# A six-layer hybrid model in one kernel: the parts of queries and keys as two float32r values in the halves of the TensorE array

## The chip, the cores and the metric

The kernel is one program on one core of a Trainium2 chip. The core has TensorE (PE) with its weight loads (PEld), VectorE (DVE), ScalarE (ACT), GpSimd (POOL) and SyncE (SP), and 16 DMA engines that the queues of SP, ACT and POOL share. The metric is the device time of one execution in microseconds (us), and the figure compared is the median of several runs. Everything is computed in this one launch.

## The reference

The input x is 2048 tokens of 128 channels. Layers are added to it one after another: softmax attention with rotary positions and a root-mean-square norm of q and k; a spline feed-forward; retention; the spline feed-forward again; linear attention; an attention with a convolution ahead of it and a mixture of four experts behind; a WKV recurrence; and the attention with experts once more. So softmax attention is computed three times and retention once. Cut to what this change touches:

```python
# softmax attention, three times: 16 heads of 8 channels, T = 2048, causal
attn = einsum('bqhd,bkhd->bhqk', q, k) * scale
attn = softmax(where(causal, attn, -inf))
out = einsum('bhqk,bkhd->bqhd', attn, v)
# retention: 16 heads, keys of 8 channels, values of 16
scores = einsum('bhtd,bhsd->bhts', q, k) * mask        # decay, causal
denom = clip(abs(scores).sum(-1), 1.0, 50000.0)
ret = einsum('bhts,bhsv->bthv', scores / denom, v)
```

## The kernel before

**Parts.** A head has only 8 channels, so its products q.k need 8 rows of the 128-row array. The kernel uses the other rows for precision: `qkv_stage` (L635) writes each transposed q and k as a sum of PARTS = 3 bfloat16 parts. ACT's `part` (L764) copies the transposed block out of PSUM as bfloat16, PE's `take_out` (L715) subtracts that copy from PSUM by a matmul with minus one, and this goes on for the second and third part; the last block's keys are cut by DVE (`keys_part`, L849). SP stores the parts to DRAM. All nine products of parts (3 x 3 x 8 = 72 = KROWS rows) are then summed by one bfloat16 matmul whose contraction runs over 128 rows: 72 of parts, two of shifts, the rest padding.

**The attention stage** (`attention_stage`, L960, about 479 us, three times) goes through 4 groups of 4 heads and 4 blocks of 512 queries, 16 units of (group, block). It has two streams. The first finds row maxima: PE's `max_unit` (L1094) makes a 128 x 512 product (`stat`, L1101) in one of three PSUM banks, and DVE's `max_unit` (L1197) reduces it, plain ones at L1209 and the diagonal ones with a mask at L1206. A bank is filled again only when DVE has left it. When a unit's maxima are there, DVE splits them in two parts, PE transposes them (L1107), and small DMAs (`load_shift_rows`, L1006) write them as two further rows of the queries, so that the next products come out already shifted. The second stream has 160 steps: per step PE makes the scores of four heads against 128 keys (`scores`, L1143, matmul L1151, two heads per PSUM tile `sc[hp]`), ACT exponentiates two heads at a time (L1087), POOL masks the diagonal (L1056), and `pv` (L1155, matmul L1164) multiplies by the values, in float32, four heads in four 32-column tiles of the array.

**The order on PE** is fixed. `attention_plan` (L917) spreads the 672 items of the first stream (the RING) evenly over the half steps; PE's loop issues, per step: wait for ACT, scores of heads 0 and 1 for the next step, its share of ring items, `pv` of the step before, wait for ACT, scores of heads 2 and 3, its share of ring items. PE issues in order, so a ring item that waits for a bank holds up everything behind it. In most units the heads of successive ring items are 0, 1, 2, 3.

**Loads.** Each group's rows come from DRAM by `load_k` and `load_q` (L95, L102) on SP's queue, the next group while a group is worked on. The first two blocks of group 0 are loaded ahead, block 0 in `qkv_stage` itself; then SP queues the other blocks, the padding of group 1 and group 1, and behind these the shift rows of the second unit.

**Retention** (`retention_heads_stage`, L1664, about 200 us) takes the heads one at a time, two buffers deep. PE makes the own (diagonal) products, 128 wide, four to a bank (L1822), and the others up to 512 wide for DVE (L1826) and up to 1024 wide for ACT (L1812); ACT and DVE sum absolute values. SP loads a head's rows by six DMAs (L1729, L1730).

Of the kernel before, what the change touches and what calls it, by code (L numbers as in the profile page):

```python
# [4 lines left out]

# [5 lines left out]
F32 = mybir.dt.float32  # L12
BF16 = mybir.dt.bfloat16
I32 = mybir.dt.int32
# [5 lines left out]
P = 128  # L20
# [6 lines left out]
PARTS = 3  # L27
KROWS = PARTS * PARTS * D
SHIFT = 2
VD = 16  # L30
HG = 4
NG = H // HG
GBUFS = 2
# [61 lines left out]
def load_k(eng, tile, k_dram, g, parts, cols, sig):  # L95

    rows = k_dram.rearrange("(g h d) a t -> g (d a) h t", h=HG, d=D)
# [4 lines left out]
def load_q(eng, tile, q_dram, g, parts, cols, sig):  # L102

    rows = q_dram.rearrange("a (g h d) c t -> a g (d c) h t", h=HG, d=D)
    for a in parts:
        eng.dma_start(tile[a * PARTS * D:(a + 1) * PARTS * D, :, cols], rows[a, g][:, :, cols]).then_inc(sig.sem, 16)

NROWS = 2 * PARTS
# [3 lines left out]
def pad_rows(eng, w, q_tile, k_tile, sig):  # L113

    for n, tile in enumerate((q_tile, k_tile)):
        eng.dma_start(tile[KROWS:P].rearrange("r h t -> r (h t)"), w["pad"][n].partition_broadcast(P - KROWS)).then_inc(sig.sem, 16)
# [23 lines left out]
def load_stage(k, d, w):  # L140

    nc = k.nc
    with ExitStack() as ctx:
# [8 lines left out]
            (w["ident"][:], d["c_ident"]),  # L152
            (w["cos"][:], d["c_cos"]),
# [4 lines left out]
        with nc.Block() as block:  # L158
# [23 lines left out]
            def _(dve):  # L182
# [4 lines left out]
                nc.vector.tensor_scalar(w["minus16"][:], w["ident"][:], -1.0, None, ALU.mult).then_inc(kept.sem, 1)  # L187
# [447 lines left out]
def qkv_stage(k, w, jobs, qkv, parts_dram, mode, turned_sb, norm, loads=(), rows=None):  # L635
# [10 lines left out]
    with ExitStack() as ctx:  # L646
# [3 lines left out]
        early = k.sb("early_parts_t", [P, 2, 2, PARTS, BANK], BF16, ctx)  # L650
        parts = [early[:, c] if c < 2 else turned_sb[:, c - 2] for c in range(NQ)]
# [33 lines left out]
        with nc.Block() as block:  # L685

            @block.tensor
            def _(pe):
# [12 lines left out]
                def turn(c):  # L701
# [4 lines left out]
                    for s in range(2):  # L706
                        nc.tensor.matmul(tp[c % 2][:, s, :], w["minus16"][:], zeros, start=True, stop=True)
# [7 lines left out]
                def take_out(c, a):  # L715

                    pe.wait_ge(cut[a].sem, cut[a].at(c + 1))
                    for s in range(2):
                        if c == NQ - 1 and s == 1:
                            pe.wait_ge(keys_cut.sem, keys_cut.at(a + 1))  # L720
                        ins = nc.tensor.matmul(tp[c % 2][:, s, :], w["minus16"][:], parts[c][:, s, a, :], start=False, stop=True, skip_group_check=True)
# [13 lines left out]
                take_out(NQ - 1, 1)  # L735

            @block.scalar
            def _(act):
# [25 lines left out]
                def part(c, a):  # L764
# [4 lines left out]
                    if c < NQ - 1:  # L769
                        ins = nc.scalar.copy(parts[c][:, :, a, :], tp[c % 2][:])  # L770
                    else:
                        ins = nc.scalar.copy(parts[c][:, 0, a, :], tp[c % 2][:, 0])
                    ins.then_inc(cut[a].sem, 1)

                for n in range(NQ):
# [3 lines left out]
                    if n > 0:  # L779
                        part(n - 1, 2)  # L780
# [5 lines left out]
                part(NQ - 1, 2)  # L786
# [5 lines left out]
            def _(dve):  # L792
# [56 lines left out]
                def keys_part(a):  # L849
# [5 lines left out]
                    nc.vector.tensor_copy(parts[NQ - 1][:, 1, a, :], tp[(NQ - 1) % 2][:, 1]).then_inc(keys_cut.sem, 1)  # L855
# [23 lines left out]
            def _(sp):  # L879
                if rows:  # L880
                    pad_rows(sp, w, *rows, padded)
                for c in range(NQ - 1 if rows else NQ):
# [5 lines left out]
                    if rows and c == 1:  # L888
                        sp.wait_ge(stored[0].sem, stored[0].at(NS))
                        load_k(sp, rows[1], parts_dram[1], 0, range(PARTS), slice(0, BANK), begun)  # L890
                        load_q(sp, rows[0], parts_dram[0], 0, range(PARTS), slice(0, BANK), begun)
                for c in range(2):
# [67 lines left out]
def attention_stage(k, w, v, parts_dram, first_rows, last_parts, scale, y, first_norm=None):  # L960
# [7 lines left out]
    ROWS = KROWS + SHIFT  # L968
    counts = []
    with ExitStack() as ctx:  # L970
        uq, uk = ([first_rows[n], k.sb(f"group_{what}", [P, HG, T], BF16, ctx)] for n, what in enumerate("qk"))
# [4 lines left out]
        mxb = k.sb("row_max_parts", [P, 2, SHIFT * HG * QC], BF16, ctx)  # L976
        mxt = k.sb("row_max_turned", [SHIFT * HG * QC, 2, P], BF16, ctx)
# [1613 lines left out]
```

## Time and profile before

| | us |
|---|---|
| median of 3 runs | 2440.61 |
| lowest and highest run | 2437.79, 2441.31 |
| the profiled execution: its span | 2438.4 |
| what lies around the span | not shown by itself; the median is 2.2 above the span |
| attention stages, PE's first to last matmul | 68.4 to 547.8, 1123.5 to 1602.5, 1840.4 to 2319.9 |
| retention heads, PE's first to last matmul | 688.0 to 888.7 |

Read the table of busy time together with the windows: an average over the whole span mixes stages with different limits. In the rows below a name such as `stat<-group_k,group_q` says which tile is written from which; PEld rows are weight loads. `first_group_q` and `group_q` are the two buffers of query rows. An "idle before" in brackets is the time the engine had stood still, and what ended it.

### The profile page before, as it was taken

To read this page: it belongs to the slowest core of one execution; us is meant where nothing else is said; L and a number is where in the kernel's file an instruction comes from. 1 tells how busy PE (TensorE), PEld (TensorE's weight loads), DVE (VectorE), ACT (ScalarE), POOL (GpSimd) and SP (SyncE) were. 2 spreads that over 40 slices of the span, in tenths; PEclk is the share of its full clock that TensorE was granted. 3 is DMA by queue.
4 is the path that set the end of the run, shared out by engine and by line. 5 is a ranking of instruction groups with operands and counts; after the bars stand their busy time and mean duration, and the time that the engine had idled before them with its cause. 6 is when DMAs were issued, how large, how long until landed. Compare 5 with 4: busy or idle time off the path is not lost. (4 is left out here: it accounts for less than half of the span.)

```text
span 2438.4 us, 38777 instructions
## 1 busy us (share of the span) xinstructions
PE 1983.5 (81%) x13002; PEld 869.3 (36%) x13002; DVE 1703.7 (70%) x4395; ACT 1355.0 (56%) x1947; POOL 419.0 (17%) x670
## 2 busy tenths in 40 slices
PE   5689999994879974777799999957555899999939
PEld 3122333223534442553223333237331223332228
DVE  6688788847567767567788888632695887888433
ACT  4246666676379965334356666732543466666812
POOL 4000021020055521310001110133000010210133
PEclk9799999996989985988899999978867999999969
DMA  7600120001111100016101010014027001100024
GB/s 199 162 1 15 27 41 1 1 1 62 52 46 48 47 16 1 1 31 188 24 1 41 9 33 1 1 45 174 23 55 188 1 3 39 41 1 1 2 93 166
DMA packets 63781, 114.82 MB, mean 47 GB/s; under 512 B 12588, under 2 KB 45486, under 8 KB 62836
## 3 DMA queue, kind: packets, MB, share of 16 engines
q1 hardware_dynamic: 55668, 98.72, 14.9%
q0 software_dynamic: 5088, 11.24, 1.6%
q10 hardware_dynamic: 2860, 2.77, 0.3%
q8 instruction: 90, 1.47, 0.3%
q14 instruction: 75, 0.61, 0.1%
HBM read 64.78 MB, written 31.56 MB: 40 GB/s over the span
## 5 line engine op out<-in xcount | busy, mean ns | idle before, releaser
L1087 ACT ACTIVATE probs<-score 128x1024 f32<-128x1024 f32 x960 | 825.7, 897 | 542.2 <-PE score L1151 539.2
L1209 DVE TENSOR_REDUCE max_part<-stat 128x1 f32<-128x512 f32 x1152 | 721.9, 683 | 113.7 <-PE stat L1101 112.2
L1164 PE MATMUL pv<-probs,v_ones 128*9 128x512 f32 (+3 forms) x3840 | 443.7, 534 | 0.7 <-ACT out_turned L1078 0.5
L1206 DVE CUSTOM_DVE_ANT_0 masked_scores<-stat,mask_row 128x128 f32<-128x128 f32 (+3 forms) x768 | 343.2, 487 | 125.7 <-PE stat L1101 124.1
L1056 POOL TENSOR_SCALAR_AFFINE_SELECT probs<-probs 128x256 f32<-128x256 f32 x384 | 154.7, 408 | 1272.5 <-ACT probs L1087 1269.1
L1101 PE MATMUL stat<-first_group_k,first_group_q 128*128 128x512 bf16 (+2 forms) x960 | 301.1, 368 | 68.2 <-DVE max_part L1209 35.7
L1101 PE MATMUL stat<-group_k,group_q 128*128 128x512 bf16 (+2 forms) x960 | 288.5, 349 | 15.1 <-DVE max_part L1209 9.1
L1151 PE MATMUL score<-first_group_q,first_group_k 128*128 128x512 bf16 x960 | 262.8, 357 | 30.1 <-DMA first_group_q<-row_max_turned 29.0
L1151 PE MATMUL score<-group_q,group_k 128*128 128x512 bf16 x960 | 254.3, 350 | 5.8 <-DMA group_q<-row_max_turned 3.5
L1101 PEld LDWEIGHTS stat<-first_group_k,first_group_q 128*128 128x128 bf16 x960 | 93.9, 99 | 250.3 <-DVE max_part L1209 123.6
L1859 ACT ACTIVATE abs_act_ps<-abs_act_ps 128x1024 f32<-128x1024 f32 (+3 forms) x176 | 167.6, 952 | 27.8 <-PE abs_act_ps L1812 27.8
L1151 PEld LDWEIGHTS score<-first_group_q,first_group_k 128*128 128x128 bf16 x960 | 73.1, 98 | 251.7 <-ACT probs L1087 107.3
L1101 PEld LDWEIGHTS stat<-group_k,group_q 128*128 128x128 bf16 x960 | 92.7, 97 | 164.8 <-DVE max_part L1209 67.7
L1151 PEld LDWEIGHTS score<-group_q,group_k 128*128 128x128 bf16 x960 | 69.4, 97 | 222.5 <-ACT probs L1087 169.7
L1893 DVE TENSOR_REDUCE abs_part<-abs_dve_ps 128x512 f32 (+5 forms) x224 | 108.6, 515 | 45.8 <-PE abs_dve_ps L1826 44.0
L2368 DVE TENSOR_TENSOR hidden<-value_ps,gate 128x512 f32<-128x512 f32 x38 | 26.3, 692 | 117.2 <-PE value_ps L2272 109.5
L1812 PE MATMUL abs_act_ps<-head_k,head_q 128*128 128x512 bf16 x352 | 100.7, 373 | 7.1 <-ACT abs_act_ps L1859 4.2
L1164 PEld LDWEIGHTS pv<-probs,v_ones 128*9 128x9 f32 x3840 | 57.3, 88 | 112.6 <-issue 90.6
L1766 POOL TENSOR_SCALAR own_positive<-own_scores 128x2048 f32<-128x2048 f32 x16 | 85.7, 5359 | 0.0
L1826 PE MATMUL abs_dve_ps<-head_k,head_q 128*128 128x512 bf16 (+2 forms) x224 | 66.4, 314 | 0.0
L1206 DVE DVE_READ_ACCUMULATOR2_ANT max_part<- 128x1 f32 x768 | 63.9, 83 | 0.1
L1232 DVE RECIPROCAL inv_denominator<-stat 128x16 f32<-128x16 f32 x48 | 12.4, 258 | 69.9 <-PE stat L1111 69.2
(369 smaller groups left out, 2318.3 us busy)
## 6 DMA issues: line engine op xcount, KB each, us to landing
tile_wv<-expert_wv SPq DMA_DIRECT2D x38, 512.0 KB
q_parts<-early_parts_t SPq DMA_DIRECT2D x20, 384.0 KB, 3.3
group_k<-k_parts SPq DMA_DIRECT2D x18, 384.0 KB
group_q<-q_parts SPq DMA_DIRECT2D x18, 384.0 KB
q_parts<-parts_t SPq DMA_DIRECT2D x17, 384.0 KB, 4.6
head_q<-q_parts SPq DMA_DIRECT2D x48, 96.0 KB
head_k<-k_parts SPq DMA_DIRECT2D x48, 96.0 KB
first_group_k<-k_parts SPq DMA_DIRECT2D x9, 384.0 KB
```

What stands on the lines that cost most here:

```text
L1056: nc.gpsimd.affine_select(tile, tile, [[0, 2], [1, P]], ALU.is_ge, 0.0, base=0, channel_multiplier=-1).then_inc(cut.sem, 1)
L1087: nc.scalar.activation(probs[:, n % PSLOTS, :, 0:width], sc[hp][:, :, 0:width], ACT.Exp, scale=scale).then_inc(expd.sem, 1)
L1101: last = nc.tensor.matmul(out[:, 0:width], uq[b][:, h, at:at + P], uk[b][:, h, c * BANK:c * BANK + width], start=True, stop=True)
L1151: last = nc.tensor.matmul(sc[hp][:, i, 0:BANK - f], uk[b][:, h, kt * P:(kt + 1) * P], uq[b][:, h, j * BANK + f:(j + 1) * BANK], start=True ...
L1164: last = nc.tensor.matmul(acc[32 * h:32 * h + D + 1, f:BANK], v9[:, kt, g * HG + h, :], probs[:, (2 * t + h // 2) % PSLOTS, h % 2, 0:BANK ...
L1206: nc.vector.tensor_tensor_reduce(masked[:, at % 2, 0:width], ring[n % RBANKS][:, 0:width], w["mask_row"][:, BANK - width:BANK], 1.0, NEG, ...
L1209: nc.vector.reduce_max(into, ring[n % RBANKS][:], AX.X).then_inc(stat_used.sem, 1)
L1766: nc.gpsimd.tensor_scalar(sa[:, par, :], sm[:, par, :], 0.0, None, ALU.max).then_inc(abs_ready.sem, 1)
L1812: ins = nc.tensor.matmul(a_ps[slot][:, b:min(b + BANK, width)], qm[:, par, i * P:(i + 1) * P], km[:, par, at + b:at + min(b + BANK, width) ...
L1826: ins = nc.tensor.matmul(out[:, 0:width], qm[:, par, i * P:(i + 1) * P], km[:, par, at:at + width], start=True, stop=True)
L1859: nc.scalar.activation(ps, ps, ACT.Abs, accum_out=part[:, bass.ds(h, 1), i, 0:1]).then_inc(a_used.sem, 1)
L1893: nc.vector.tensor_reduce(part[:, bass.ds(h, 1), i, slot:slot + 1], d_ps[n % DRING][:, 0:width], AX.X, ALU.add, apply_absolute_value=True) ...
```

## The change

PARTS goes from 3 to 2, and a part is now a float32 whose value was rounded to the matmul type float32r (4 bytes an element). KROWS becomes 2 x 2 x 8 = 32, which with the two shift rows fits in 64 rows. So two heads share a 128-row tile, one in each half, and each product is a matmul over 64 rows of the array. In the attention stage head h lies in half h % 2. In retention each head is loaded twice, into both halves, and successive matmuls take the halves in turn (four own products of one bank stay in one half).

What goes with it: the third part's copy, subtraction and store fall away; the subtraction is a float32r matmul; each group is loaded by 8 DMAs (was 6), its shift rows are cleared by 2 (was 1) and the padding set by 4 (was 2); a retention head is loaded by 8 DMAs (was 6) of 128 KB (was 96 KB), and its padding is set by 8 memsets over 32 partitions (was 4 over 64). The three early blocks of parts have a buffer of their own that ends with `qkv_stage`, so SP waits there until the third block's stores have landed too (was the first two). The padding comes from a DRAM buffer filled in `load_stage`. The transposed maxima are float32. In the diff F32R is float32r.

```diff
-PARTS = 3
+PARTS = 2
 KROWS = PARTS * PARTS * D
+HROWS = 64
+PAIRS = HG // 2
+def rounded(ap):
+    return ap.bitcast(F32R)
+def head_rows(h):
+    return slice(HROWS * (h % 2), HROWS * (h % 2) + HROWS)
 def load_k(...):        # load_q alike
-    for a in parts:
-        eng.dma_start(tile[a * PARTS * D:(a + 1) * PARTS * D, :, cols], rows[g][:, :, cols]).then_inc(sig.sem, 16)
+    for i in range(2):
+        for a in range(PARTS):
+            at = HROWS * i + a * PARTS * D
+            eng.dma_start(tile[at:at + PARTS * D, :, cols], rows[g, i][:, :, cols]).then_inc(sig.sem, 16)
...
 # qkv_stage, PE (and on ACT part(n - 1, 2) and part(NQ - 1, 2) go)
                     turn(n)
-                    if n > 0:
-                        take_out(n - 1, 1)
                     if n + 2 < NQ:
                         project(n + 2)
                     take_out(n, 0)
-                take_out(NQ - 1, 1)
 # qkv_stage, SP
-                for c in range(2):
+                for c in range(NQ - 1):
                     sp.wait_ge(stored[c].sem, stored[c].at(NS))
...
 # attention_stage, PE: max_unit and scores
-                    last = nc.tensor.matmul(out[:, 0:width], uq[b][:, h, at:at + P], uk[b][:, h, c * BANK:c * BANK + width],
-                                            start=True, stop=True)
+                    rows = head_rows(h)
+                    last = nc.tensor.matmul(out[:, 0:width], rounded(uq[b][rows, h // 2, at:at + P]), rounded(uk[b][rows, h // 2, c * BANK:c * BANK + width]),
+                                            start=True, stop=True, tile_position=(rows.start, 0))
-                        last = nc.tensor.matmul(sc[hp][:, i, 0:BANK - f], uk[b][:, h, kt * P:(kt + 1) * P], uq[b][:, h, j * BANK + f:(j + 1) * BANK],
-                                                start=True, stop=True)
+                        rows = head_rows(2 * hp + i)
+                        last = nc.tensor.matmul(sc[hp][:, i, 0:BANK - f], rounded(uk[b][rows, hp, kt * P:(kt + 1) * P]),
+                                                rounded(uq[b][rows, hp, j * BANK + f:(j + 1) * BANK]), start=True, stop=True, tile_position=(rows.start, 0))
...
 # retention_heads_stage, SP
-                    for a in range(PARTS):
-                        at = slice(a * PARTS * D, (a + 1) * PARTS * D)
+                    for e in range(SIDES):
+                        for a in range(PARTS):
+                            at = slice(HROWS * e + a * PARTS * D, HROWS * e + (a + 1) * PARTS * D)
 # PE: one `rows = next(sides)` ahead of each "a" matmul and of each "d" bank
+                    sides = itertools.cycle(head_rows(e) for e in range(SIDES))
-                                ins = nc.tensor.matmul(a_ps[slot][:, b:min(b + BANK, width)], qm[:, par, i * P:(i + 1) * P],
-                                                       km[:, par, at + b:at + min(b + BANK, width)], start=True, stop=True)
+                                rows = next(sides)
+                                ins = nc.tensor.matmul(a_ps[slot][:, b:min(b + BANK, width)], rounded(qm[rows, par, i * P:(i + 1) * P]),
+                                                       rounded(km[rows, par, at + b:at + min(b + BANK, width)]), start=True, stop=True, tile_position=(rows.start, 0))
```

## Rows read from the trace of the kernel before

**Rows 1.** The page's part 1: busy us, share of span, instructions.

```profile
PE 1983.5 (81%) x13002; PEld 869.3 (36%) x13002; DVE 1703.7 (70%) x4395; ACT 1355.0 (56%) x1947; POOL 419.0 (17%) x670
```

**Rows 2.** Windows: four of the second attention stage, one of two retention heads.

```profile
core 0: us, PE busy (x) PEld busy (x) DVE busy (x) ACT busy (x) POOL busy (x), PEclk, DMA share, GB/s
1137.40:1169.90 32.50, 17.65 (x70) 5.13 (x69) 19.30 (x54) 5.49 (x8) 3.27 (x8) 0.76 0.76 156
1169.90:1510.00 340.10, 321.18 (x1945) 100.27 (x1943) 286.68 (x738) 205.87 (x244) 35.29 (x88) 0.99 0.08 15
1510.00:1593.80 83.80, 81.41 (x535) 24.12 (x538) 50.44 (x148) 64.06 (x76) 9.43 (x25) 1.00 0.01 1
761.30:785.90 24.60, 23.85 (x241) 11.54 (x240) 18.76 (x41) 22.63 (x47) 12.89 (x6) 1.00 0.13 48
1123.40:1602.50 479.10, 437.31 (x2640) 134.77 (x2640) 368.28 (x992) 291.14 (x354) 53.48 (x129) 0.97 0.13 29
```

**Rows 3.** Timeline of one step; columns: start us, us, engine, line, what.

```profile
1468.42 3.18 DVE L1209 TENSOR_REDUCE max_part<-stat 128x1 f32<-128x512 f32 x5
...
1469.87 0.10 PEld L1101 LDWEIGHTS stat<-group_k,group_q 128*128 128x128 bf16 x1 [0.41 <-DVE max_part L1209]
...
1470.19 1.04 PE L1164 MATMUL pv<-probs,v_ones 128*9 128x512 f32 x8
...
1471.17 0.60 PE L1151 MATMUL score<-first_group_q,first_group_k 128*128 128x512 bf16 x2
...
1471.61 0.59 PE L1101 MATMUL stat<-group_k,group_q 128*128 128x512 bf16 x2
...
1472.03 1.29 DVE L1209 TENSOR_REDUCE max_part<-stat 128x1 f32<-128x512 f32 x2 [0.42 <-PE stat L1101]
1472.04 0.59 PE L1151 MATMUL score<-first_group_q,first_group_k 128*128 128x512 bf16 x2
...
1473.09 0.62 PE L1164 MATMUL pv<-probs,v_ones 128*9 128x512 f32 x4
```

**Rows 4.** Three lines' loads and matmuls: count, duration ns min/median/max, starts, forms.

```profile
L1101 PEld LDWEIGHTS stat<-first_group_k,first_group_q x960: 95/97/152, 68.3 to 2173.9; 128*128 128x128 bf16 x192
...
L1111 PEld LDWEIGHTS stat<-ident,out_turned x192: 138/141/146, 131.6 to 2319.5; 128*128 128x128 f32 x192
L1111 PE MATMUL stat<-ident,out_turned x192: 272/273/328, 131.8 to 2319.6; 128*128 128x128 f32 x192
...
L2272 PEld LDWEIGHTS gate_ps<-sorted_t,tile_wv x304: 192/192/338, 1660.4 to 2429.5; 128*128 128x128 f32 x152
L2272 PE MATMUL gate_ps<-sorted_t,tile_wv x304: 274/275/582, 1660.4 to 2429.6; 128*128 128x128 f32 x152
```

**Rows 5.** Timeline of PE where four transposes are issued.

```profile
1441.43 0.60 PE L1111 MATMUL stat<-ident,out_turned 128*128 128x128 f32 x4
1441.87 0.54 PE L1101 MATMUL stat<-first_group_k,first_group_q 128*128 128x512 bf16 x2
```

**Rows 6.** Timeline of PE, linear layer: four products in 32-row tiles.

```profile
1024.88 1.14 PE L1488 MATMUL tile_scores_ps<-tile_q_heads,tile_k_t 32*128 32x512 f32 x8
```

**Rows 7.** Groups by line, DVE: count, busy us, mean ns, idle before.

```profile
L1209 DVE TENSOR_REDUCE max_part<-stat 128x1 f32<-128x512 f32 x1152 | 721.9, 683 | 113.7 <-PE stat L1101 112.2
```

**Rows 8.** Waits from 1132 to 1172 us: us in total, times, longest.

```profile
PE score L1151 <- DMA first_group_q<-row_max_turned: 8.8, 1, 8.8
```

**Rows 9.** Timelines of SP's queue and ACT before the second attention stage.

```profile
1119.44 1.79 SPq L126 DMA_DIRECT2D q_parts<-parts_t  x3
1121.28 1.34 SPq L131 DMA_DIRECT2D k_parts<-parts_t  x1
...
1111.70 1.02 ACT L770 CAST early_parts_t<-turned_qk 128x1024 bf16<-128x1024 f32 x1
```

**Rows 10.** Timelines, retention: head 0's last load, four 128-wide products.

```profile
681.48 0.70 SPq L1730 DMA_DIRECT2D head_k<-k_parts  x1
...
761.37 0.40 PE L1822 MATMUL abs_dve_ps<-head_q,head_k 128*128 128x128 bf16 x4
```

More of the change, by code:

```diff
@@ L13 @@
 BF16 = mybir.dt.bfloat16
+F32R = mybir.dt.float32r
 I32 = mybir.dt.int32
@@ L115, in pad_rows @@
     for n, tile in enumerate((q_tile, k_tile)):
-        eng.dma_start(tile[KROWS:P].rearrange("r h t -> r (h t)"), w["pad"][n].partition_broadcast(P - KROWS)).then_inc(sig.sem, 16)
+        for i in range(2):
+            rows = tile[HROWS * i + KROWS:HROWS * i + HROWS].rearrange("r p t -> r (p t)")
+            eng.dma_start(rows, w["pad"][n].partition_broadcast(HROWS - KROWS)).then_inc(sig.sem, 16)
 def parts_stored(k):
@@ L706, in turn @@
                     for s in range(2):
-                        nc.tensor.matmul(tp[c % 2][:, s, :], w["minus16"][:], zeros, start=True, stop=True)
+                        nc.tensor.matmul(tp[c % 2][:, s, :], w["ident16"][:], zeros, start=True, stop=True)
                     pe.wait_ge(ready.sem, ready.at(c + 1))
@@ L1106, in shift_unit @@
                     rows = SHIFT * HG * QC
-                    nc.tensor.transpose(ring[n % RBANKS][0:rows, 0:P // 2].bitcast(BF16), mxb[:, u % 2, :], w["ident16"][:]).then_inc(stat_full.sem, 1)
+                    nc.tensor.transpose(ring[n % RBANKS][0:rows, 0:P], mxb[:, u % 2, :], w["ident"][:]).then_inc(stat_full.sem, 1)
                 def out_unit(n, u):
@@ L1226, in shift_unit @@
                     rows = mxt.shape[0]
-                    nc.vector.tensor_copy(mxt[:, u % 2, :], ring[n % RBANKS][0:rows, 0:P // 2].bitcast(BF16)).then_inc(stat_used.sem, 1)
+                    nc.vector.tensor_copy(mxt[:, u % 2, :], ring[n % RBANKS][0:rows, 0:P]).then_inc(stat_used.sem, 1)
                 def out_unit(n, u):
@@ L1248, in attention_stage @@
         for sig in padded:
-            sig.done(2 * 16)
+            sig.done(NPADS * 16)
         for b in range(GBUFS):
@@ L1252, in attention_stage @@
         for b in range(GBUFS):
[L1253 removed]
+            cleared[b].done(2 * 16 * (NG // GBUFS - 1))
         for sig in shift_in:
@@ L1449, in chunk_stage, with _ @@
         with nc.Block() as block:
+            if not inner:
+                @block.sync
+                def _(sp):
+                    wait_parts(sp, parts_stored(k))
             @block.gpsimd
@@ L1703, in retention_heads_stage @@
         stored = parts_stored(k)
-        PADDED = slice(64, P)
-        NL = 2 * PARTS * 16
+        SIDES = 2
+        PADDED = tuple(slice(HROWS * e + KROWS, HROWS * (e + 1)) for e in range(SIDES))
+        NL = 2 * PARTS * SIDES * 16
         q_rows = parts_dram[0][:, :, 0, :].rearrange("a (h d) t -> h a d t", d=D)
@@ L1723, in body @@
                         sp.wait_ge(d_full.sem, d_full.at(h * NV - NV))
[L1724 to L1730 removed]
+                    for e in range(SIDES):
+                        for a in range(PARTS):
+                            at = slice(HROWS * e + a * PARTS * D, HROWS * e + (a + 1) * PARTS * D)
+                            sp.dma_start(qm[at, par, :], bcast(q_rows[h, a], 0, PARTS)).then_inc(loaded[par].sem, 16)
+                            sp.dma_start(km[at, par, :], k_rows[h]).then_inc(loaded[par].sem, 16)
                 wait_parts(sp, stored)
@@ L1817, in body @@
                             pe.wait_ge(d_used.sem, d_used.at(h * NV + (n + 1 - DRING)))
-                        out = d_ps[n % DRING]
+                        out, rows = d_ps[n % DRING], next(sides)
                         if n < ND:
@@ L1870, in _ @@
                 for par in range(2):
-                    nc.vector.memset(qm[PADDED, par, :], 0.0).then_inc(q_padded.sem, 1)
+                    for rows in PADDED:
+                        nc.vector.memset(qm[rows, par, :], 0.0).then_inc(q_padded.sem, 1)
                 dve.wait_ge(cleared.sem, cleared.at(1))
@@ L1907, in retention_heads_stage @@
         cleared.done(5)
-        q_padded.done(2)
-        k_padded.done(2)
+        q_padded.done(4)
+        k_padded.done(4)
         a_full.done(NA * H)
@@ L2564, in shape_constants @@
         "c_qdecay": tiles(np.exp(gamma * (pos - T // 2)) / np.sqrt(decay_sum)),
-        "c_pad": np.repeat(np.array([[0], [0xBF80BF80]], dtype=np.uint32), HG * T // 2, axis=1).view(np.float32),
+        "c_pad": np.repeat(np.array([[0.0], [-1.0]], dtype=np.float32), PAIRS * T, axis=1),
         "c_kdecay": tiles(np.exp(gamma * (T // 2 - pos))),
```

134 lines of the change are left out of this document (66 added, 68 removed).

## The prediction

> **What bounds the kernel now.** I read the page's busy shares first: PE 81%, DVE 70% [rows 1], an average over stages with different limits. The windows come next. The attention stage takes 479.1 us and there are three alike, so the time is decided there: PE 437.3 busy, DVE 368.3, ACT 291.1 [rows 2]. Its stretches differ. In the first, 32.5 us, PE is half idle. In the second, units 1 to 11, 340.1 us for 116 steps, PE is busy 321.2 and DVE 286.7: DVE stands still 53.4 us, 0.46 a step. In the third, units 12 to 14, 83.8 us for 36 steps, PE is busy 81.4, DVE only 50.4, ACT 64.1.
>
> The timeline of one step shows how the two hold each other [rows 3]. DVE ends five reductions at 1468.42 + 3.18 = 1471.60 and starts again at 1472.03, 0.42 idle. The loop behind it: the last ring product before `pv` is released by DVE at 1469.87 (PE had waited 0.41 for a bank); `pv` starts at 1470.19, 0.32 later; the scores at 1471.17, 0.98 later; the first new ring product at 1471.61, 0.44 later; its result reaches DVE 0.42 later. That is 2.16 us, in which DVE has three filled banks, 1.73 us of work. The step, `pv` to `pv`, is 1473.09 - 1470.19 = 2.90. So neither engine alone is the bound: the step is DVE's four reductions plus an idle time that PE's serial work between two fillings of a bank makes.
>
> **The change, part by part.**
>
> *Two heads side by side.* In row tiles of the array, four float32 products of 512 columns are done in 1.14 us as eight records [rows 6]; the transposes show a 4-byte record of 128 columns every 0.11 us [rows 5], 0.44 for 512, and eight in a row would take 3.5. So products in different row groups do overlap, 4 bytes wide too. The pair of scores after `pv` then takes 0.22 where it takes 0.44. DVE's idle time falls from 0.42 to 0.20, the step by 0.22. The other pair of scores, and ring products side by side, gain nothing here: behind them PE waits for a bank, 0.41 in the row, and only waits longer. What is late next is DVE with its four reductions of 0.61 (two in 1.29 less one of 0.68) [rows 3, 7]. Of the 116 steps 44 are diagonal, with scores 512, 384, 256 and 128 wide, 320 in the mean: 0.216 x 72 + 0.133 x 44 = 21.4 us a stage.
>
> In units 12 to 14 PE works nearly without a gap, so both pairs count: 0.43 x 24 + 0.27 x 12 = 13.5 us. ACT limits this to 83.8 - 64.1 = 19.7, and ring items still hold PE in unit 12; I take 9 of the 13.5, and with the weights below 6 (bounds 2 and 13).
>
> *Weights.* A load of 128 bfloat16 columns takes 97 ns, of 4-byte ones 141 in a transpose and 192 in a plain float32 matmul [rows 4]. A load ahead of a running matmul hides. It shows twice a step: at the first scores after `pv`, and at the last ring product, which waits for DVE with its load. The trace has no float32r; the load with one record per instruction, 141, is nearest: 0.044 x 2 = 0.088 a step, 116 x 0.088 = 10.2 us. The bounds are 0 and, at 192, 22.
>
> The Trainium skill (TensorE: Matmul & The Clock Gate, Weight-path perf modes) speaks against the change here: fast weight load works only for types other than FP32, and an ordinary load takes columns / 1.2 ns, 107 for 128. The trace agrees on the order, 97 against 141. Were the whole difference to a quarter of that exposed, 80 ns, the stage would pay 19 instead of 10, and the sum would be about 26 us higher.
>
> *Columns.* I take one column a cycle, as with bfloat16, for 256 columns and more. The only single-record 4-byte matmul, the transpose, goes at half of that, 0.11 for 128 columns [rows 5], and the plain float32 one makes two such records an instruction (304 for 152) [rows 4], 0.22. These are the bounds, and half rate is a rival below, because the transpose also has to carry all 32 bits. 
> For 128-wide products I take the transpose's 0.11 instead of 0.056: 64 ring and 64 score products a stage, +0.053 each, 6.8 us of PE of which a third is on the path, 2 us. Bounds 0 and, at 0.22, about 10.
>
> Sum per attention stage: -21.4 + 10.2 - 6 + 2 = -15, three times -45 us.
>
> *The first 45 us of the stage* stay. Unit 1 starts when its shift rows land, after PE has idled 8.8 us [rows 8]; they lie behind the other blocks, the padding and group 1 in the same queues. That was 6 x 192 + 2 x 896 + 6 x 384 = 5248 KB, and becomes 8 x 128 + 4 x 512 + 8 x 256 = 5120 KB: at the window's 156 GB/s [rows 2] 34 us and 33.6. Six more issues of some 0.4 us on SP are hidden under that transfer. If the rates shift by a fifth it is up to 7 us a stage either way.
>
> *Parts.* Per `qkv_stage` the third part's copies go, 1.02 us each on ACT [rows 9], with the subtraction between them. They are not the end: SP's queue is, issuing the stores of block 2 until 1121.28 + 1.34 = 1122.62, and the attention stage opens at once [rows 9]. SP issues one store less and two loads more, and starts some 3 us earlier, since the last part of a block is ready earlier. Against it stands the new wait for block 2's stores to land, with a transfer of about 5 us by the page, and the end of the block, hence all engines, behind it. I take 0; bounds -3 and +4 for each of four stages.
>
> *Retention.* Two heads take 24.6 us: ACT is busy 22.6, PE 23.9 [rows 2]. ACT caps the gain at 1.0 a head, 16 us in all. Overlapping 512-wide products take up to 3 us of PE a head away, the 20 products of 128 columns (four in 0.40 with their latency [rows 10]) bring back 20 x 0.053 = 1.1, or 3.3 at the upper bound. I take half of the cap, -8 us; bounds -14 and +12. The heads are still loaded in time, 8 issues of some 0.8 us in a 12.3 us head; head 0 starts later by two issues of 0.70 [rows 10], +2 with the larger transfers. GpSimd's and DVE's padding memsets lie beside that load. Net -6.
>
> *Smaller.* The maxima go through a float32 transpose, 0.05 us longer, 16 times a stage; the padding copied through DRAM is one more issue at the start. Nothing.
>
> Sum: 2438.4 - 45 - 6 = 2387. The traced execution lies 2.2 us below the median of the runs, so I predict 2390, 2.1% faster. TensorE's granted clock is 1.0 from unit 2 on and 0.76 in the first stretch, where PE is half idle [rows 2]; with about a fifth less PE work it stays far above that load.
>
> **Rivals.**
>
> 1. *The halves take turns.* Float32r products in two halves do not overlap, though the float32 tiles of rows 6 did. Then the 0.22 is gone while weights (0.088 x 152 = 13 a stage) and narrow products (4) stay: +17 three times, and in retention, where PE is the busiest engine, 20 x 0.053 + 0.3 = 1.4 a head, +24 with the start. 2440 + 75 = 2515. It decides from the point where the overlap of a pair is under 0.09 us. For it: only plain float32 is shown in row tiles. Against it: nothing in those rows depends on the number of passes. 14%.
> 2. *Half rate.* 4-byte columns stream at two cycles each, as in the transpose. A pair then takes 0.44 as today, and the last and the first ring product, which stand alone, 0.21 longer each: with the weights 0.52 a step, 0.4 in the mean with the narrow ones, about 60 a stage; in retention about 1.4 a head. 2440 + 180 + 25 = 2645. 9%.
> 3. *Weights eat it.* The load costs what it does in a float32 matmul, 192: 0.19 a step instead of 0.088, 22 against 21.4, and in units 12 to 14 nothing is left. Retention about even: 2440, 2430 to 2455. For it: the waiting product's load is visible in every step. 12%.
> 4. *The stages open later*: the wait for block 2's stores or slower loads to 16 partitions cost 7 us or more in each. 2390 + 25 = 2415. 5%.
>
> **How the numbers follow.** The forecast 60%, rivals 14, 9, 12 and 5. The forecast's own range, from its bounds, is 2355 to 2425 (weights fully hidden at one end, narrow products at 0.22 and retention +12 at the other). To hold 8 in 10 the range takes in rivals 3 and 4 and not 1 and 2: 2350 to 2475. A change within 0.2%, 5 us, cannot be told from none. Faster: 0.60 + 0.05 and a third of rival 3, less a little for the forecast's edge, 0.67; same 0.06; slower 0.27.
>
> **What would show it.** In the changed trace: score matmuls of a pair some 10 ns apart (right) or 216 and more (rival 1), and successive products in one half 0.216 apart (right) or 0.43 (rival 2); weight loads of scores near 141 (right) or 192 (rival 3); a full step of units 1 to 11 near 2.77 where 2.90 stands, DVE's idle time there about 0.28; 128-wide products of one bank 0.11 apart; ACT near 95% busy in retention. The prediction is wrong if units 1 to 11 take more than 335 us or less than 320.

## The result and the profile after

The median of 4 runs is 2629.07 us (2617.4 to 2636.8) against 2440.8 before: a ratio of 1.077, 95% interval 1.073 to 1.080. The change makes the kernel 7.7% slower; I had forecast 2.1% faster, 2390, in a range of 2350 to 2475.

The page of the changed kernel, busy times and granted clock in 40 slices:

```profile
PE 2063.9 (78%) x12963; PEld 1083.7 (41%) x12970; DVE 1716.4 (65%) x4393; ACT 1345.8 (51%) x1931; POOL 421.9 (16%) x672
...
PEclk8579999997756656688658999996967689999969
```

PE's busy time has grown although its products are fewer and go in pairs [rows 1], and the clock row has slices of 5 to 8 in retention and at the start of each attention stage. A busy time is no measure of work where the clock moves. By stage, PE's first to last matmul, in us:

| us | before | after | difference |
|---|---|---|---|
| three attention stages | 479.5, 479.0, 479.5 | 497.3, 506.6, 497.5 | +63 |
| retention heads | 200.7 | 324.3 | +124 |
| end of the stage ahead to retention's first product | 11.3 | 23.7 | +12 |
| all the rest | | | -5 |
| span | 2438.4 | 2632.3 | +194 |

Windows of the changed kernel: the lead-in (maxima only, ahead of the first scores) with unit 0, unit 1, unit 2, units 3 to 11, and retention.

```profile
core 0: us, PE busy (x) PEld busy (x) DVE busy (x) ACT busy (x) POOL busy (x), PEclk, DMA share, GB/s
67.90:117.60 49.70, 33.79 (x98) 17.36 (x98) 31.42 (x103) 8.71 (x11) 5.07 (x9) 0.53 0.84 149
117.60:157.90 40.30, 37.46 (x155) 15.49 (x154) 30.20 (x74) 14.37 (x18) 3.20 (x8) 0.67 0.00 1
157.90:210.00 52.10, 48.76 (x219) 19.34 (x218) 39.38 (x91) 22.14 (x26) 2.89 (x8) 0.76 0.00 1
210.00:475.60 265.60, 238.50 (x1574) 95.33 (x1573) 218.54 (x573) 168.66 (x202) 28.77 (x73) 1.00 0.13 18
713.20:1037.50 324.30, 258.83 (x1920) 174.40 (x1920) 154.44 (x318) 188.86 (x368) 106.85 (x48) 0.58 0.12 49
```

The same five windows of the kernel before (the prediction had cut the stage otherwise):

```profile
68.40:115.20 46.80, 27.59 (x97) 7.89 (x98) 30.63 (x103) 8.75 (x11) 5.07 (x9) 0.72 0.76 176
115.20:149.50 34.30, 29.37 (x155) 8.64 (x153) 29.98 (x74) 14.20 (x17) 3.27 (x8) 0.95 0.00 1
149.50:193.80 44.30, 39.59 (x220) 11.78 (x217) 39.51 (x92) 22.32 (x26) 3.22 (x8) 1.00 0.00 1
193.80:455.30 261.50, 252.13 (x1574) 79.81 (x1573) 217.20 (x574) 169.30 (x201) 28.77 (x72) 1.00 0.10 20
688.00:888.70 200.70, 192.46 (x1920) 93.72 (x1920) 150.79 (x318) 181.95 (x368) 106.95 (x48) 0.99 0.12 44
```

Of the 18 us that the attention stage loses, 17 lie in the first three lines, where the clock is 0.53 to 0.76 instead of 0.72 to 1.00. In units 3 to 11, at full clock, it is 4 us longer, and the end of the stage gives 3 back. Units 1 to 11 take 358.0 us; the prediction had named more than 335 as its sign of being wrong. Retention has the clock at 0.58, and something else. Its waits, from 715 to 1030 us (us in total, times, longest):

```profile
SPq L1749 <- PE abs_act_ps L1839: 198.0, 14, 18.4
...
PE abs_dve_ps L1849 <- DMA head_k<-k_parts: 62.1, 15, 8.0
```

and its transfers from 735 to 800 us, with the rate in 40 slices:

```profile
GB/s 60 55 50 50 60 60 50 50 50 60 50 50 50 50 60 50 50 60 50 60 50 50 50 40 55 55 50 50 55 50 60 50 50 60 50 50 50 55 55 50
DMA packets 471, 3.46 MB, mean 53 GB/s; under 512 B 52, under 2 KB 52, under 8 KB 52
...
head_k<-k_parts SPq DMA_DIRECT2D x12, 128.0 KB
```

The queue never pauses, and never moves more than 60 GB/s. The share of the DMA engines in retention is 0.12 to 0.13, which is two of sixteen. Eight transfers of 128 KB are 1.05 MB a head, 19.8 us at 53 GB/s, and a head takes 20.3 (324.3 / 16). Before, a head's loads ran at 79 GB/s while they lasted (share 0.20 from 714.5 to 721.5 us, three of sixteen), and the queue then rested; 712 to 737 us of the kernel before:

```profile
GB/s 0 0 20 0 79 85 59 79 79 79 79 79 105 72 79 79 13 0 0 0 0 0 20 0 59 79 79 79 79 92 79 79 79 79 79 79 26 0 0 0
```

A full step of unit 11 (answers to [rows 3]):

```profile
445.88 0.19 PEld L1171 LDWEIGHTS score<-first_group_q,first_group_k 64*128 64x128 f32 x2 [0.86 <-ACT probs L1106]
445.88 0.50 PE L1171 MATMUL score<-first_group_q,first_group_k 64*128 64x512 f32 x2
445.99 0.19 PEld L1121 LDWEIGHTS stat<-group_k,group_q 64*128 64x128 f32 x2
446.21 0.40 PE L1121 MATMUL stat<-group_k,group_q 64*128 64x512 f32 x2
446.45 0.39 PE L1171 MATMUL score<-first_group_q,first_group_k 64*128 64x512 f32 x2
446.65 2.48 DVE L1229 TENSOR_REDUCE max_part<-stat 128x1 f32<-128x512 f32 x4 [0.68 <-PE stat L1121]
447.39 0.50 PE L1121 MATMUL stat<-group_k,group_q 64*128 64x512 f32 x1 [0.32 <-DVE max_part L1229]
447.82 1.05 PE L1184 MATMUL pv<-probs,v_ones 128*9 128x512 f32 x8
448.80 0.50 PE L1171 MATMUL score<-first_group_q,first_group_k 64*128 64x512 f32 x2
```

Pairs do run side by side: from 446.21 on a pair of 512 columns starts every 0.23 us, where two products took 0.43. But the step, 448.80 - 445.88, is 2.92, and was 2.90. The loop of the prediction, in its order: last ring product to `pv` 0.43 (was 0.32), `pv` to scores 0.98 (0.98), scores to ring product 0.33 (0.44), to DVE 0.44 (0.42), together 2.18 (2.16). The load at 445.99 starts 0.11 after the one ahead of it, and the pair behind it 0.33 after the waiting pair instead of 0.23. I read this as 0.11 of the waiting products' own weight load that nothing hides; experiment 6 tests it. The loads themselves:

```profile
L1121 PEld LDWEIGHTS stat<-first_group_k,first_group_q x960: 182/186/336, 67.9 to 2370.0; 64*128 64x128 f32 x192
```

186 ns in the median, against 97 [rows 4].

### The profile page after: what moved, and what is told of

It is laid out like the page before. It is cut to its first block and busy times, and to the rows that moved or that the text cites. A ratio compares the mean times of both kernels' runs of the same rounds, so it can differ in the third digit from the quotient of the medians.

```text
span 2632.3 us, 38781 instructions
## 1 busy us (share of the span) xinstructions
PE 2063.9 (78%) x12963; PEld 1083.7 (41%) x12970; DVE 1716.4 (65%) x4393; ACT 1345.8 (51%) x1931; POOL 421.9 (16%) x672
## 5 line engine op out<-in xcount | busy, mean ns | idle before, releaser
L1121 PE MATMUL stat<-first_group_k,first_group_q 64*128 64x512 f32 (+3 forms) x960 | 359.5, 503 | 64.6 <-DVE max_part L1229 29.9
L1121 PE MATMUL stat<-group_k,group_q 64*128 64x512 f32 (+2 forms) x960 | 300.6, 400 | 52.7 <-DVE max_part L1229 35.1
L1171 PE MATMUL score<-first_group_q,first_group_k 64*128 64x512 f32 x960 | 249.5, 470 | 33.1 <-DMA first_group_q<-row_max_turned 30.1
L1121 PEld LDWEIGHTS stat<-first_group_k,first_group_q 64*128 64x128 f32 x960 | 179.1, 227 | 212.6 <-DVE max_part L1229 120.7
L1171 PEld LDWEIGHTS score<-first_group_q,first_group_k 64*128 64x128 f32 x960 | 115.3, 209 | 246.5 <-issue 141.0
L1171 PE MATMUL score<-group_q,group_k 64*128 64x512 f32 x960 | 209.7, 431 | 8.5 <-DMA group_q<-row_max_turned 3.7
L1121 PEld LDWEIGHTS stat<-group_k,group_q 64*128 64x128 f32 x960 | 145.3, 189 | 149.4 <-DVE max_part L1229 93.5
L1171 PEld LDWEIGHTS score<-group_q,group_k 64*128 64x128 f32 x960 | 93.7, 185 | 206.1 <-ACT probs L1106 167.5
L1839 PE MATMUL abs_act_ps<-head_k,head_q 64*128 64x512 f32 x352 | 147.0, 683 | 1.8 <-ACT abs_act_ps L1886 1.5
L1853 PE MATMUL abs_dve_ps<-head_k,head_q 64*128 64x512 f32 (+2 forms) x224 | 96.7, 489 | 0.0
```

Of the source, the lines that this page charges most:

```text
L1121: last = nc.tensor.matmul(out[:, 0:width], rounded(uq[b][rows, h // 2, at:at + P]), rounded(uk[b][rows, h // 2, c * BANK:c * BANK + width] ...
L1171: last = nc.tensor.matmul(sc[hp][:, i, 0:BANK - f], rounded(uk[b][rows, hp, kt * P:(kt + 1) * P]), rounded(uq[b][rows, hp, j * BANK + f:(j ...
L1839: ins = nc.tensor.matmul(a_ps[slot][:, b:min(b + BANK, width)], rounded(qm[rows, par, i * P:(i + 1) * P]), rounded(km[rows, par, at + b:at ...
L1853: ins = nc.tensor.matmul(out[:, 0:width], rounded(qm[rows, par, i * P:(i + 1) * P]), rounded(km[rows, par, at:at + width]), start=True, st ...
```

## The experiments

I supposed three causes. The rows theory: the halves use 64 of 128 rows, and with 64 rows at work TensorE's clock stays at 1.2 GHz. The loads theory: retention's loads are paced by two DMA engines. The weights theory: the float32r weight loads eat the overlap. Each is taken away by itself below. The recorded expectations also call the first one the clock theory; its rival there, the type theory, has the number type hold the clock down. Times are medians of 4 runs, ratios against the kernel before, and stages are PE's first to last matmul.

**1. Retention's rows in another order.**

```diff
-        q_rows = parts_dram[0][:, :, 0, :].rearrange("a (h d) t -> h a d t", d=D)
-        k_rows = parts_dram[1].rearrange("(h d) a t -> h a d t", d=D)
+        q_rows = parts_dram[0].rearrange("a (h d) c t -> h a (d c) t", d=D)
+        k_rows = parts_dram[1].rearrange("(h d) a t -> h (d a) t", d=D)
...
-                            sp.dma_start(qm[at, par, :], bcast(q_rows[h, a], 0, PARTS)).then_inc(loaded[par].sem, 16)
+                            sp.dma_start(qm[at, par, :], q_rows[h, a]).then_inc(loaded[par].sem, 16)
```

(The second copy of q is not stored in this layer, so these rows hold old values: only the times count here.)

> The changed kernel, with one thing altered: a retention head's rows are loaded with the head dimension outermost (one run of 16 rows per transfer instead of 2 x 8), so that the same 1 MB per head comes in eight transfers of the same size. Loads theory (the retention stage is paced by its loads, 1 MB a head at the 53 GB/s of two DMA engines, 19.8 us, where the head takes 20.2): the transfers spread over more than two engines, PE's waits for head_k (86 us) go, the stage falls from 324 us on PE to 190 to 215, and the total from 2629 to 2485 to 2510. Clock theory (products over 64 of the 128 rows make the chip hold TensorE at 1.2 GHz, and that paces the head): the loads come earlier, but the stage stays above 300 us with the clock at 0.5 to 0.66, total 2610 or more.

Measured: 2533.8 us, 1.037 (1.036 to 1.039). PE no longer waits for a load, and the stage takes 240.2 us:

```profile
708.10:948.30 240.20, 234.76 (x1920) 157.36 (x1920) 152.98 (x318) 185.35 (x368) 107.13 (x48) 0.69 0.50 65
```

The DMA share went from 0.12 to 0.50, and the queue now rests between heads; 735 to 800 us:

```profile
DMA  0299791000007999900006999900029998500999
GB/s 0 81 161 146 96 146 15 0 0 10 0 0 161 116 126 111 131 5 10 0 0 161 116 126 116 126 0 0 0 81 161 116 126 96 66 0 0 197 126 116
```

While it loads, nine tenths of the sixteen engines are busy, but they move mostly 110 to 160 GB/s, two to three times the 53 of two engines and not eight times. Why each moves less isn't shown. So the loads had cost 84 us in the stage, and 12 us ahead of it (the gap there is 11.9 again, not 23.7). But 240 is above the 190 to 215 that the loads theory gave: PE is busy 98% of the time and its clock is 0.69. Neither theory holds alone.

**2. Retention's heads loaded once, all products in the first half.**

```diff
-        SIDES = 2
+        SIDES = 1
...
```

> The changed kernel with a retention head loaded once and all its products in the first 64 rows: 512 KB a head instead of 1 MB, over the same two DMA engines, and no products side by side. Loads theory: 9.8 us of transfer fit into a head of 12.3 us, so the stage falls to about 200 to 225 us and the total to 2490 to 2520, although the overlap of the halves is gone. Clock theory: the rows in use are still 64, so the clock stays near 0.55 and the stage above 300; total 2610 or more. If the overlap itself is worth much here, this one is clearly slower than the run with the rows in another order.

Measured: 2664.5 us, 1.091 (1.088 to 1.094), slower than the change itself; the stage takes 369.4 us. One 50 us window in it, and the whole stage:

```profile
780.00:830.00 50.00, 50.00 (x276) 36.48 (x273) 21.45 (x42) 26.48 (x50) 15.59 (x7) 0.50 0.06 25
...
708.10:1077.50 369.40, 368.42 (x1920) 274.14 (x1920) 165.21 (x318) 194.55 (x368) 106.93 (x48) 0.50 0.05 21
```

This is the clearest window of the study. PE is busy all of it, it waits for no load, and the clock stands at 0.50, its lower level of 1.2 GHz, for 369 us. The loads theory's 200 to 225 us fell here, the clock theory's "above 300" stood: a busy TensorE isn't enough.

**3. Full rows in retention.** Each head is loaded once, as in experiment 2, but the products run over all 128 rows, the last 96 of them zeros in both operands.

```diff
-        SIDES = 2
+        SIDES = 1
-                    sides = itertools.cycle(head_rows(e) for e in range(SIDES))
+                    sides = itertools.cycle([slice(0, P)])
-        PADDED = tuple(slice(HROWS * e + KROWS, HROWS * (e + 1)) for e in range(SIDES))
+        PADDED = (slice(KROWS, HROWS), slice(HROWS, P))
... (and each product without its `tile_position`)
```

> The changed kernel, but a retention head is loaded once (512 KB, same order of rows as there) and its float32r products use all 128 rows of the array, of which the last 96 hold zeros in both operands. Beside the run with 64 rows and one load only the number of rows in use differs. Rows theory (the clock stays at 1.2 GHz in that stage because only 64 rows are in use at a time): granted clock near 1.0, 12.5 to 13.5 us a head, PE's stage 200 to 220 us instead of 369, total 2500 to 2520. Type theory (float32r products keep the clock low, whatever the rows): clock 0.5 as there, stage above 330, total 2630 or more.

Measured: 2519.2 us, 1.033 (1.032 to 1.035). Beside the last run the rows that a product spans differ, and with them its `tile_position`:

```profile
702.20:921.70 219.50, 216.71 (x1920) 159.29 (x1920) 152.91 (x319) 185.17 (x368) 107.27 (x48) 0.98 0.09 36
```

Clock 0.98 and 219.5 us for 0.50 and 369.4. The number type is the same in both, so it isn't what holds the clock down here; the rows spanned are, and zeros in them are enough. Whether it is the rows themselves or the array's being addressed in halves, no run here separates: every 64-row product has a `tile_position`, no 128-row one has. The 219.5 is also what float32r costs retention with neither halves nor late loads: 19 us over bfloat16's 200.7, PE busy 99%.

**4. Full rows with the double loads.** All loads are as in the changed kernel; the products run over both copies at once, which gives twice the scores, so only the times count.

```diff
-                    sides = itertools.cycle(head_rows(e) for e in range(SIDES))
+                    sides = itertools.cycle([slice(0, P)])
... (and each product without its `tile_position`)
```

> The changed kernel with every load as it is (a head loaded twice, 1 MB in eight transfers of 2 x 8 rows), but the retention products use all 128 rows at once, both copies, so that they give twice the scores (the output is not the reference's). Against the run with full rows and one load, which took 219.5 us, only the loads differ. Loads theory (1 MB a head over two engines at 53 GB/s bounds the stage by itself): about 19.8 us a head, stage 310 to 325, whatever the clock; total 2610 to 2635. Clock theory (with all rows in use the stage is free of its trouble, the waits for loads being only a consequence of late starts): 215 to 240, total 2515 to 2545.

Measured: 2626.3 us, 1.077 (1.075 to 1.079):

```profile
712.60:1037.30 324.70, 272.14 (x1920) 209.42 (x1920) 160.43 (x318) 188.97 (x368) 106.93 (x48) 0.78 0.12 49
```

324.7 us, to 0.4 us what the changed kernel takes (324.3), at a clock of 0.78 instead of 0.58. So in the changed kernel the loads alone set this stage, and the low clock is hidden behind them. Experiment 1 took the cover away and showed it. The clock is also 0.78 here and 0.98 in experiment 3, with the same products over full rows: PE now stands still for 50 us, waiting for loads. So of the fall from 0.99 to 0.58 in the changed kernel's retention a part goes with the waits, and only the rest with the halves.

**5. Full rows in the attention stage.** Every product gives the sum of two heads' scores, and the shift row's -1 is made -0.5; only the times count.

```diff
-... rounded(uq[b][rows, h // 2, at:at + P]), rounded(uk[b][rows, h // 2, c * BANK:c * BANK + width]), ..., tile_position=(rows.start, 0))
+... rounded(uq[b][:, h // 2, at:at + P]), rounded(uk[b][:, h // 2, c * BANK:c * BANK + width]), start=True, stop=True)
```

and the same for the scores.

> The changed kernel with its retention as it is, and in the attention stages every score and ring product uses all 128 rows, so that it computes the sum of the two heads' scores (with the shift halved; the output is not the reference's). Loads, types, columns and order are the same, only no halves. Rows theory: in units 0 to 2 the clock is 0.77 and more instead of 0.54 to 0.73, and they take 113 to 118 us instead of 128.6. Type theory: 126 or more. In the steady steps nothing pays for the float32r weights: a full step of 3.05 to 3.15 us where 2.92 stands, an attention stage of 510 to 520 us, total 2660 to 2700. If the overlap had been worth nothing, the stage would stay at 500 or less.

Measured: 2676.0 us, 1.096 (1.095 to 1.098), stage 513.9. The lead-in with unit 0, unit 1, unit 2, and units 3 to 11:

```profile
67.20:116.80 49.60, 34.09 (x97) 18.94 (x97) 31.49 (x103) 8.72 (x10) 5.05 (x9) 0.64 0.83 150
116.80:152.60 35.80, 33.43 (x156) 16.20 (x155) 30.14 (x74) 14.43 (x17) 3.25 (x8) 0.95 0.01 1
152.60:199.60 47.00, 44.73 (x219) 21.71 (x218) 39.79 (x92) 22.47 (x26) 3.20 (x8) 1.00 0.00 1
199.60:482.20 282.60, 278.31 (x1574) 143.40 (x1573) 218.89 (x573) 170.30 (x202) 29.13 (x72) 1.00 0.13 17
```

Units 1 and 2 have the clock of the kernel before again, 0.95 and 1.00, and take 82.8 us instead of 92.4, without any overlap. That part of the rows theory holds. Units 0 to 2 take 118.8 us, just over its 113 to 118 and well under the type theory's 126. The lead-in with unit 0 is unchanged (49.6 us, clock 0.64 for 0.53), so its 3 us over the kernel before are not the rows'; what they are isn't shown. A full step is 3.15, the upper end of what I expected, and 0.23 above the 2.92 with halves:

```profile
461.47 1.05 PE L1184 MATMUL pv<-probs,v_ones 128*9 128x512 f32 x8
464.62 1.04 PE L1184 MATMUL pv<-probs,v_ones 128*9 128x512 f32 x8
```

And rows are not all there is to the clock: in the changed kernel's units 3 to 11 the scores and ring products span 64 rows too, with `pv` over 128 rows between them, and the clock is 1.00.

**6. bfloat16 in the halves, attention only.** Three bfloat16 parts, but only the six products with the largest parts, 48 rows; the DRAM buffers hold them in six slots, so that a group's half is one transfer of 48 rows. Retention loads two such transfers a head and keeps full-array products.

```diff
-KROWS = PARTS * PARTS * D
+SLOTS6 = PARTS * (PARTS + 1) // 2
+KROWS = SLOTS6 * D
+HROWS = 64
...
-... uq[b][:, h, at:at + P], uk[b][:, h, c * BANK:c * BANK + width], start=True, stop=True)
+... uq[b][head_rows(h), h // 2, at:at + P], uk[b][head_rows(h), h // 2, c * BANK:c * BANK + width],
+    start=True, stop=True, tile_position=(head_rows(h).start, 0))
```

> The kernel before, with attention in halves but in bfloat16: of the nine products of parts the six large ones are kept (high-high, high-middle, high-low, middle-high, middle-middle, low-high), 48 rows a head and two heads in the 64-row halves. Retention keeps full-array products and bfloat16, its head's 48 rows in two transfers. Weights theory (the float32r load, exposed by about 0.11 us twice a step, ate the 0.22 us of the overlap): with bfloat16 loads of 97 ns the full step falls from 2.91 to 2.70 us, units 3 to 11 by 15 to 20 us a stage. Rival (the overlap gives nothing, since the ring is paced elsewhere): the step stays at 2.88 or more. The clock of units 0 to 2: if rows in use decide it, these units take 122 to 130 us as in the changed kernel, total about 2410; if the number type does, 113, total about 2375.

Measured: 2361.6 us, 0.967 (0.966 to 0.969): the fastest kernel here and 3.3% under the one before. The attention stage takes 452.8 us. A step, then unit 1 and units 3 to 11:

```profile
410.15 0.39 PE L1164 MATMUL score<-first_group_q,first_group_k 64*128 64x512 bf16 x2
410.16 0.10 PEld L1114 LDWEIGHTS stat<-group_k,group_q 64*128 64x128 bf16 x2
410.37 0.38 PE L1114 MATMUL stat<-group_k,group_q 64*128 64x512 bf16 x2
...
412.83 0.39 PE L1164 MATMUL score<-first_group_q,first_group_k 64*128 64x512 bf16 x2
```
```profile
108.40:144.30 35.90, 30.68 (x155) 6.79 (x153) 29.87 (x73) 14.22 (x17) 3.27 (x8) 0.76 0.00 1
...
189.50:437.80 248.30, 214.48 (x1574) 54.15 (x1573) 216.51 (x574) 168.89 (x202) 29.04 (x73) 0.99 0.08 14
```

The next load starts 0.01 after the waiting products, not 0.11, the pair behind them 0.22 after and not 0.33, and the step is 2.68. The weights theory holds. What changed is the type as a whole, but the columns stream as fast in both (0.22 and 0.23 us for 512), so the load is what is left in a full step. The clock of unit 1 is 0.76 and not 0.95, with bfloat16 too: rows again. Yet unit 1 is only 1.6 us longer than before. The total is below both figures that I gave, and units 0 to 2 take 105.5 us where I had 122 to 130 or 113: the lead-in with unit 0, 38.8 us instead of 46.8, had been left out of them. It moves 5.2 MB instead of 8.2 (rate times window), so about 8 of the 27 us that the stage gains look like the smaller loads' and not the halves'; no run parts the two.

With experiment 5 this makes a table of two by two, units 3 to 11 (96 steps), all at a clock of 0.99 or 1.00:

| | one product at a time, 128 rows | pairs in halves |
|---|---|---|
| bfloat16 | 261.5 | 248.3 |
| float32r | 282.6 | 265.6 |

Halves give 13 to 17 us, float32r takes 17 to 21. In a full step alone it is 2.90 and 2.68 with bfloat16, 3.15 and 2.92 with float32r.

**7. bfloat16 in the halves in retention too.**

```diff
-        SIDES = 1
+        SIDES = 2
...
```

with the products' rows alternating as in the change.

> The bfloat16 kernel with six products of parts, and now the retention heads in the halves too: 48 rows loaded twice (four transfers a head), row products alternating halves. Rows theory: the clock falls in the retention stage to 0.6 to 0.9 although nothing is float32r; a head takes 12.8 to 14.5 us, the stage 205 to 235 (201 with full rows), total 2365 to 2395. Type theory: the clock stays at 1.0, the overlap gives PE 1 to 3 us a head and ACT limits the stage to 190 to 196; total 2352 to 2357.

Measured: 2365.8 us, 0.970 (0.968 to 0.973), the stage 199.7 us:

```profile
667.40:867.10 199.70, 177.80 (x1920) 83.77 (x1920) 151.08 (x318) 181.19 (x368) 106.93 (x48) 0.86 0.30 58
```

Against 200.6 with full rows in experiment 6 the halves give 0.9 us. The clock fell to 0.86, as the rows theory has it, but my price for that was too high: 205 was its lower end. PE's busy time is down to 177.8, so it has slack, and ACT is 91% busy, the busiest engine of the stage.

**8. More full-array work to lift the clock.** In experiment 6's kernel, the first 100 ring products get a product over all 128 rows ahead of them, overwritten at once.

```diff
+                    if n < FILL:
+                        nc.tensor.matmul(out[:, 0:width], uq[b][:, h // 2, at:at + P], uk[b][:, h // 2, c * BANK:c * BANK + width], start=True, stop=True)
```

> The bfloat16 kernel with attention in halves, and ahead of each of the first 100 ring products of a stage (units 0 and 1) one more product over all 128 rows into the same bank, overwritten at once by the real one: more work for TensorE, no change in the result. Rows theory: the full-array work brings the clock of the first 80 us of the stage from 0.52 to 0.76 up to 0.9 or more, units 0 and 1 take 50 to 57 us instead of 60.3, total 2340 to 2355. Rival (the clock doesn't answer to it, the added 0.2 to 0.4 us a product only lengthens the ring's loop): units 0 and 1 take 70 us or more, total 2390 or more.

Measured: 2425.8 us, 0.994 (0.993 to 0.996), 64 us slower than without. Two windows:

```profile
69.30:100.00 30.70, 28.32 (x76) 7.32 (x76) 17.55 (x62) 6.64 (x6) 3.49 (x5) 0.50 0.67 158
100.00:150.00 50.00, 49.39 (x203) 13.17 (x202) 36.12 (x85) 11.67 (x14) 2.03 (x5) 0.85 0.05 8
```

In the first 31 us PE is 92% busy and the clock is still 0.50; the kernel before had 0.77 in its first 31.6 us with PE 75% busy. The added products only take their own time. Later the clock is 0.85 (0.76 in experiment 6's window from 100 to 150), too late. The rival was right. Why the clock doesn't rise at the start with full rows in every second product stays open.

## Why the prediction was wrong

**Retention, +136 us with its start where I had -6.** The failed step is "The heads are still loaded in time, 8 issues of some 0.8 us in a 12.3 us head". I counted issues and not bytes at a rate. Before, 6 x 96 KB at 79 GB/s took 7.5 us of a 12.3 us head; the change makes it 8 x 128 KB. Even at the old rate that is 13 us, more than a head: the rows shown for the stage had the 48 GB/s and the period [rows 2]. And the rate itself fell to 53 GB/s, as the outer dimension of a load went from three parts to two. Experiments 1 and 4 show it from both sides. Rival 4 named "slower loads to 16 partitions", as 7 us or more in each attention stage. The 8 us that the overlap was to give in retention are not there either: in experiment 7 it gives 0.9. Only the price of the narrow products was right: in experiment 3 the 128-wide ones follow each other every 0.11 us, and the stage is 19 us over bfloat16's, where 16 heads of 1.1 make 17.

The Trainium skill (DMA: Bandwidth & Descriptors, Why a DMA increments its semaphore by 16 and not by 1) has the rule: a transfer is spread over the largest number of engines, up to 16, that divides the slowest dimension of both sides. The slowest dimension of a retention load is PARTS on the DRAM side, so by it PARTS = 3 gives three engines and PARTS = 2 two, and the 16 merged rows of experiment 1 sixteen. The trace agrees: shares of 0.20, of 0.12 to 0.13, and of nine tenths while the merged loads run. I had not weighed it.

**The clock.** "With about a fifth less PE work it stays far above that load" failed in both kinds of stage. I took PE's work alone for what keeps the clock up. In units 1 and 2 of the attention stage PE is 93% busy, more than the 88% before, and the clock is lower; with full rows it is back, and the two units take 9.6 us less (experiment 5). In retention it is 240 against 219.5 once PE no longer waits for loads (experiments 1 and 3, of which the first still loads twice the bytes); with products in one half only, 150 us (experiments 2 and 3). The Trainium skill (TensorE: Matmul & The Clock Gate, Part 1: The HAM clock gate) ties the full clock to a busy engine. The trace disagrees for products over 64 rows: busy 368.4 of 369.4 us at 0.50.

**Weights, 17 us over 96 steps, in proportion 21 over 116, where I had 10.** (Narrow products are in it.) The step "the load with one record per instruction, 141, is nearest" took the wrong row. A float32r load takes 186, as a plain float32 one's 192, and exposes 0.11 more than bfloat16's, twice a step, not 0.044. This is rival 3: it forecast even, and units 3 to 11 are 4 us from even. The estimate that I had worked out from the Trainium skill (TensorE: Matmul & The Clock Gate, Weight-path perf modes), 80 ns exposed and 19 us a stage, was the better guide.

**The overlap, right.** I had -0.22 a full step, 21.4 us for 116 steps. With bfloat16 the step fell by 0.22 (2.90 to 2.68), with float32r by 0.23 (3.15 to 2.92), and the halves give 13 to 17 us over 96 steps, where my rate makes 18. Rivals 1 and 2 are out: the products of a pair start 3 ns apart in the records, and at full clock pair follows pair at 0.23, near one column a cycle (0.21) and far from two.

**Units 12 to 14** gained 2.8 us (83.8 to 81.0) where I had 6, the lower end of my bounds; with bfloat16 7.5. **Opening of the stages**: ahead of the second and third attention stage `qkv_stage` is 1.5 us shorter on PE and the gap behind it 1.1 to 1.7 longer; my 0 holds.

The first attention stage adds up: lead-in and unit 0 +2.9, units 1 and 2 +13.8 (of it 9.6 rows, and 4.2 that experiment 5 has too), units 3 to 11 +4.1, units 12 to 14 -2.8, together +18. The second stage lost 28; its clock dipped once more later (0.82 from 1400 to 1450 us), and why then isn't shown. The five runs with this same attention code have stages of 493.5 to 506.9 us, where the kernel before has 479.0 to 479.5.

## What to carry to other kernels

Price a load by its bytes over the rate of the engines it will be spread on, taken from a row of the profile, since sixteen engines did not move eight times what two did. Look at the outermost dimension of both sides when a constant such as PARTS changes. Take the number of array rows that a product spans as part of what keeps TensorE's clock up: a product over 64 rows streams as many columns as one over 128 and saves nothing by itself, and without a partner in the other half it may run at half the clock. Where a pair of products in halves is to gain, keep the type whose weight load is fast, since an engine that waits shows part of every load; fewer, chosen partial products in bfloat16 did here what two float32r parts were to do.

## What the hardware showed

- Retention with its score products over 64 rows, all in one half, PE 100% busy: granted clock 0.50 for 369 us (experiment 2); the same over 128 rows, 96 of them zeros: 0.98 (experiment 3). Products alternating between the halves: 0.69 with float32r (experiment 1), 0.86 with bfloat16 (experiment 7).
- float32r: 512 columns in 0.23 us at full clock (changed kernel), 128 columns with new weights each every 0.11 us (experiment 3), a 128-column weight load 186 ns (bfloat16 95, experiment 6).
- A load with an outer dimension of 2 has a DMA share of two engines in sixteen and 53 GB/s (changed kernel); with 3, of three and 79 GB/s (kernel before); with 16, nine tenths and mostly 110 to 160 GB/s (experiment 1).
